# Order of work on four engines: roundings, idle matmuls, row sums and window sums moved in a two-layer attention and convolution kernel

## The chip, the cores and the metric

The kernel runs on one core of a Trainium2 chip. Its time is the device time of one execution in microseconds; the median of several executions is used for comparisons. One more execution is taken with the hardware profiler; its span, from the first to the last instruction, is a little shorter than its time.

## What is computed

Four images of 256 channels by 32 x 32 go through two residual layers, each behind a group normalisation. Layer 0 is attention: 4 heads within windows of 2 x 2 pixels (`hifi`), and 4 heads in which each pixel attends to the 256 pooled windows (`lofi`). Layer 1 is a 3 x 3 convolution of an image that is multiplied by a mask; the mask is made from weighted row and column sums of the image.

```python
qkv = (xw @ h_qkv_w)...                       # window attention, 2 x 2 pixels
attn = softmax(einsum('bghnd,bghmd->bghnm', q, k) * SCALE)
hifi = (attn @ v) @ h_proj_w + h_proj_b
q = xh @ l_q_w; kv = pooled @ l_kv_w          # attention to pooled windows
attn = softmax(einsum('bnhd,bmhd->bhnm', q, k) * SCALE)
lofi = (attn @ v) @ l_proj_w + l_proj_b
x = x + L0(gn(x))
mask = 1 - (|posX - mu_x| + |posY - mu_y|) * mask_weight   # mu from row and column sums
x = x + conv3x3(relu(gn(x) * max(mask, -1))) + bias
```

## The kernel before

Each engine has its own instruction list, written out by hand, and waits on semaphores. SyncE's queue (SP) issues all DMAs. PSUM is held in four pairs of banks: `slot[0]`, `slot[1]`, `slot[2]` for attention, `cps` for the convolution (in the first image, where there is no convolution yet, `cps` serves attention too). Most matrices are multiplied as a high and a low part: ScalarE rounds to the high part, and VectorE or GpSimd subtracts it to give the low part.

For each image b there is a front and a rest. `front(b)` on TensorE: the projection of the local queries; four idle matmuls in image 1 (`keep_warm(WARM[10])`); the pooled keys and values; the window projections with the group means of image b-1 between them; then eight blocks n of local products (`qs` by `ks`, L1180 on), block n into `slot[LA_SLOT[n]]`, from block 3 on only when `la_max` says that the maximum three blocks back is taken. Behind each block stand some matmuls of the previous image's convolution (`conv.more(FRONT[..])`) or, in image 1, idle matmuls on `cps` (`WARM[1 + n]`: 6, 1 and 2 behind blocks 5, 6 and 7). Then follow the turning (a transpose) of the maxima `l_max`, the window sums (`window_scores`, 16 matmuls), the turning of these sums, and the first two score tiles. The convolution of image b-1 begins behind that. `rest(b)` makes the other score tiles, the window values, the head sums (`by_head` with ones), the window output projection, the head products, idle matmuls in image 0 (`WARM[9]`), and the output projection of the local part, which waits for VectorE's product `lnorm` (L917). The convolution of image b-1 fills all gaps from image 1's rest on.

VectorE in a front: the queries' low part (`query_lo`, L771), the keys' low part (`key_lo`, L776, which waits for ScalarE), the row sums (L675) and column sums (L676 to L681) of image b-1, its normalisation (L637 and L610 to L623, behind TensorE's group means), the mask rows (`mask_parts`), the eight maxima (L782), the maxima's high and low parts (`maxima_parts`, L790), the masked images (L722), the first convolution tiles (L736), the window softmax (L799 to L806), more tiles, and the tiles' low parts (L752), for which the convolution waits. In a step: four value products (L885), two adds and a third (L892, L893, L896), the next image's normalisation, transposes (L909), and the product L917.

ScalarE in a front: rectifies the first masked image (L503), copies the window sums to SBUF (L542), rectifies the second, then the softmax's exponential and the tiles' high parts. In image 0's step it takes the exponentials of score tiles 0 to 3 (L520), waits for GpSimd's turned convolution weights (`cw_pool`), rounds two of them (`weight_high`, L461), and then takes the exponentials of tiles 4 to 7.

GpSimd: the window products q by k (L348), which start behind the mask rows of image b-1, the mask sums (L333), and parts of the convolution weights (L374 to L377, and L315 behind ScalarE's two roundings).

## Time and profile before

| | us |
|---|---|
| median of 3 runs (lowest, highest) | 368.33 (368.22, 368.52) |
| profiled execution, its own time | 366.82 |
| its span | 364.9 |
| busy: TensorE, VectorE, ScalarE, GpSimd | 322.0, 280.5, 148.0, 85.8 |
| mean granted TensorE clock, share of full | 0.949 |

A busy TensorE is not one at its peak, since ends of matmuls are modelled. All times of rows are microseconds from the start of the span unless a column says ns. The stretches are: image 0's front and step to about 78 us, image 1's front to about 123, then fronts and steps with the convolution of the previous image between them, some 76 us an image, and from about 305 us the last image's convolution.

### The profile page before, as it was taken

The numbers are of one execution on the slowest core, as the hardware profiler recorded it, in microseconds if no ns is written. First come the engines' busy times: TensorE is split into PE (matmuls) and PEld (weight loads), VectorE is DVE, ScalarE is ACT, GpSimd is POOL, SyncE is SP. The second block draws the span as 40 slices with busy tenths as digits, with TensorE's granted clock in tenths as the row PEclk, the third lists the DMA queues.
The fourth block names the chain that finished last, engine by engine and source line by source line (L and its number), as shares of the span: only waits on it lengthen the run. The fifth ranks groups of instructions, "written<-read, shape, count | busy, mean of one in ns | idle before, by whom it ended". The sixth has DMA issues, their size and how long they took to land.

```text
span 364.9 us, 4118 instructions
## 1 busy us (share of the span) xinstructions
PE 322.0 (88%) x1546; PEld 227.9 (62%) x1546; DVE 280.5 (77%) x518; ACT 148.0 (41%) x186; POOL 85.8 (24%) x47
## 2 busy tenths in 40 slices
PE   1786864999797699998999999998999999979995
PEld 1375542257564485486868773786777836858884
DVE  4979839777867957789897877988879847997662
ACT  2443556345443635535215764453048333031300
POOL 0464948000192020000760020005900200202000
PEclk9999698799968599999899999998999999999999
DMA  8659700007900000029510300098001000101002
GB/s 266 259 81 129 238 5 0 2 0 98 118 2 4 0 2 1 0 82 129 63 38 25 115 3 0 2 169 105 2 4 57 3 0 0 59 0 57 2 0 117
DMA packets 10340, 20.39 MB, mean 56 GB/s; under 512 B 1872, under 2 KB 4816, under 8 KB 10064
## 3 DMA queue, kind: packets, MB, share of 16 engines
q1 hardware_dynamic: 10320, 20.13, 26.8%
q8 instruction: 12, 0.20, 0.2%
q14 instruction: 8, 0.07, 0.1%
HBM read 7.93 MB, written 4.19 MB: 33 GB/s over the span
## 4 chain that ended last, share of the span: by engine, by line
PE 58%; DVE 17%; DMA 8%; ACT 6%; issue 4%; SPq 2%; POOL 2%; DVEq 0%
PE slot L1003 26%; PE cps L1035 16%; PE slot L1079 7%; DMA ks<-probs 4%; PE cps L1003 4%; DMA qs<-probs 3%; ACT probs L520 2%; PE cps L1079 2%; SPq L257 1%; DVE v_lo L752 1%; DVE xn L979 1%; SPq L261 1%; DVE l_max L782 1%; DMA xy<-x 1%; PE slot L1206 1%
## 5 line engine op out<-in xcount | busy, mean ns | idle before, releaser
L348 POOL TENSOR_TENSOR probs<-q_w,k_w 128x1024 f32<-128x1024 f32 x16 | 38.4, 2428 | 115.7 <-DVE rw L715 110.5
L1035 PE MATMUL cps<-v_hi,cw_hi 128*128 128x512 f32 (+1 forms) x144 | 58.6, 407 | 3.8 <-DVE v_lo L752 3.6
L1035 PE MATMUL cps<-v_hi,cw_lo 128*128 128x512 f32 (+1 forms) x144 | 58.4, 406 | 0.0
L1035 PE MATMUL cps<-v_lo,cw_hi 128*128 128x512 f32 (+1 forms) x144 | 57.4, 398 | 0.0
L782 DVE TENSOR_REDUCE l_max<-slot 128x4 f32<-128x1024 f32 x32 | 37.6, 1219 | 7.2 <-PE slot L1003 7.2
L520 ACT ACTIVATE probs<-slot 128x1024 f32<-128x1024 f32 x32 | 31.9, 1023 | 16.8 <-PE slot L1003 16.7
L1035 PEld LDWEIGHTS cps<-v_hi,cw_hi 128*128 128x128 f32 x144 | 28.3, 197 | 14.2 <-ACT v_hi L514 4.3
L1003 PE MATMUL slot<-ks,qs 96*128 96x256 f32 x128 | 24.9, 343 | 10.5 <-DVE l_max L782 4.4
L1035 PEld LDWEIGHTS cps<-v_hi,cw_lo 128*128 128x128 f32 x144 | 28.0, 194 | 6.3 <-issue 0.7
L1035 PEld LDWEIGHTS cps<-v_lo,cw_hi 128*128 128x128 f32 x144 | 28.1, 195 | 4.9
L1003 PEld LDWEIGHTS slot<-ks,qs 96*128 96x128 f32 x128 | 21.8, 236 | 14.4 <-DVE l_max L782 6.7
L503 ACT ACTIVATE xn<-mask 128x1024 f32<-128x1024 f32 x8 | 8.5, 1058 | 45.5 <-DVE mask L722 45.5
L1003 PE MATMUL slot<-xn_hi,w_hi 128*128 128x512 f32 x60 | 24.7, 411 | 2.3 <-DVE xn_lo L650 2.3
L333 POOL TENSOR_TENSOR mask<-rw 128x1024 f32<-128x1024 f32 x8 | 15.2, 1915 | 44.3 <-DVE rw L715 44.3
L1003 PE MATMUL slot<-qs,ks 98*128 98x512 f32 x64 | 21.0, 421 | 5.1 <-ACT probs L520 3.5
L514 ACT CAST v_hi<-mask 128x1024 fp32r<-128x1024 f32 x16 | 16.8, 1049 | 21.0 <-DVE mask L744 11.8
L1003 PE MATMUL slot<-xn_hi,w_lo 128*128 128x512 f32 x60 | 23.9, 398 | 0.0
L1003 PE MATMUL slot<-xn_lo,w_hi 128*128 128x512 f32 x60 | 23.7, 394 | 0.0
L392 POOL TENSOR_TENSOR q_w<-q_w,k_w 128x1024 f32<-128x1024 f32 x3 | 7.2, 2416 | 67.2 <-DVE k_w L885 67.2
L1003 PE MATMUL slot<-probs,cst 128*32 128x512 f32 x176 | 22.8, 657 | 0.0
L752 DVE TENSOR_TENSOR v_lo<-mask,v_hi 128x1024 fp32r<-128x1024 f32 x16 | 19.2, 1224 | 2.3 <-ACT v_hi L514 2.3
L1003 PE MATMUL cps<-cst 128*128 128x384 f32 x44 | 19.7, 602 | 0.0
(188 smaller groups left out, 623.2 us busy)
## 6 DMA issues: line engine op xcount, KB each, us to landing
qs<-probs SPq DMA_DIRECT2D x24, 256.0 KB, 7.5
xy<-x SPq DMA_DIRECT2D x8, 512.0 KB, 8.1
out<-xy SPq DMA_DIRECT2D x8, 512.0 KB, 2.8
raw_cw<-conv_w SPq DMA_DIRECT2D x2, 1152.0 KB, 6.9
ks<-probs SPq DMA_DIRECT2D x12, 128.0 KB, 7.4
probs<-h_qkv SPq DMA_DIRECT2D x2, 192.0 KB, 4.5
probs<-l_kv SPq DMA_DIRECT2D x2, 128.0 KB, 3.9
probs<-selectors SPq DMA_DIRECT2D x1, 256.0 KB, 4.0
```

Source lines behind the costliest of these rows:

```text
L257: sp.dma_start(qs[HD * part:HD * (part + 1), :, n].bitcast(F32), parts[:, n].bitcast(F32)).then_inc(done, 16)
L333: nc.gpsimd.tensor_tensor(mask[:, k].rearrange("p (h w) -> p h w", h=H), rw[:, k, 0].unsqueeze(2).to_broadcast([P, H, W]), rw[:, k, 1].uns ...
L348: nc.gpsimd.tensor_tensor(qk[:, j].rearrange("p (n w) -> p n w", n=NW), q_w[:].rearrange("p (n w) -> p n w", n=NW), k_w[:, j * G:(j + 1) * ...
L392: nc.gpsimd.tensor_tensor(pv[0], pv[0], pv[1], ALU.add).then_inc(pv_pool, 1)
L503: nc.scalar.activation(xn[:, k], mask[:, k], ACT.Relu).then_inc(relu, 1)
L514: nc.scalar.copy(v_hi[:, k, 2 * phase:2 * phase + 2].rearrange("p a b -> p (a b)"), mask[:, k]).then_inc(v_act, 1)
L520: nc.scalar.activation(probs[:, i], flat[score_slot(b, i)], ACT.Exp, scale=SCALE / NW)\
L752: nc.vector.tensor_tensor(v_lo[:, k, part].rearrange("p a b -> p (a b)"), mask[:, k], v_hi[:, k, part].rearrange("p a b -> p (a b)").bitca ...
L782: nc.vector.tensor_reduce(l_max[:, bass.ds(n, HEADS, step=NB)], flat[LA_SLOT[n]].rearrange("p (h m) -> p h m", h=HEADS), AX_X, ALU.max, ne ...
L1003: return nc.tensor.matmul(dst, lhsT, rhs, start=start, stop=stop)
L1035: ins = nc.tensor.matmul(cps[:, pos % 2, y0 * WT:y1 * WT], (cw_hi, cw_hi, cw_lo)[part][:, k, pos, dy + 1, o * P:(o + 1) * P], (v_hi, v_lo, ...
L1079: ins = nc.tensor.matmul(last_bank(o, pos)[:, y0 * WT:y1 * WT], (cw_hi, cw_hi, cw_lo)[part][:, k, pos, dy + 1, o * P:(o + 1) * P], (v_hi, ...
```

## The change

- ScalarE, image 0: the two roundings (`weight_high(1, ...)`, with their wait for GpSimd) follow the exponentials of tiles 4 to 7 instead of preceding them.
- `WARM` is cut to three numbers: 5 at the start, 1 instead of 4 behind image 0's head products, 4 ahead of image 1's pooled keys; those behind the blocks of image 1's front are gone (6, 1 and 2).
- Blocks 5 to 7 of the local products use `slot[0]` and `slot[1]` alone, so each waits for the maximum two blocks back (`LA_FREE`). The window sums go to `slot[2]` (to `cps` in image 0) ahead of the turning of the maxima, which goes to `slot[1]`.
- ScalarE copies the window sums ahead of both rectifications.
- The row sums are an operation of their own (`row_sums`, semaphore `rows_c`): ahead of the keys' low part in image 1's front, behind it in later ones.

```diff
-LA_SLOT = (0, 1, 2, 0, 1, 2, 0, 1)
+LA_SLOT = (0, 1, 2, 0, 1, 0, 1, 0)
+LA_FREE = (0, 0, 0, 1, 2, 4, 5, 6)
-WARM = (5, 0, 0, 0, 0, 0, 6, 1, 2, 4, 4)
+WARM = (5, 1, 4)
...
-                if not first:
-                    rectify(b - 1, 0)
                 act.wait_ge(ssum_pe, b + 1)
-                nc.scalar.copy(q_w[:], flat_cps if first else flat[0]).then_inc(ssum_sb, 1)
-                if not first:
-                    rectify(b - 1, 1)
+                nc.scalar.copy(q_w[:], flat_cps if first else flat[2]).then_inc(ssum_sb, 1)
+                if not first:
+                    for k in range(KT):
+                        rectify(b - 1, k)
...
                     exp_scores(b, range(2, LT - NW))
-                    act.wait_ge(cw_pool, CW_TURNED)
-                    weight_high(1, V_SUM, 2)
-                    weight_high(1, V_DIFF, 0)
...
                 exp_scores(b, range(LT - NW, LT))
+                if first:
+                    act.wait_ge(cw_pool, CW_TURNED)
+                    weight_high(1, V_SUM, 2)
+                    weight_high(1, V_DIFF, 0)
...
-            def line_sums(b, at=slice(0, KT), done=mask_c):
+            def row_sums(b, at=slice(0, KT)):
 
                 carry()
+                n = at.stop - at.start
+                y = img(b, at.start, 0, n * HW).rearrange("p (k h w) -> p k h w", k=n, h=H)
+                nc.vector.tensor_reduce(rc[:, at, 0], y, AX_X, ALU.add).then_inc(rows_c, 1)
...
-                rows = slot[2][0:NB * HEADS, 0, 0:P]
+                rows = slot[1][0:NB * HEADS, 0, 0:P]
...
-                    key_lo(b)
+                    for early in (True, False):
+                        if early == (older is None):
+                            dve.wait_ge(y_ready, b * KT)
+                            row_sums(b - 1)
+                        if early:
+                            key_lo(b)
...
-                        pe.wait_ge(la_max, b * NB + n - 2)
+                        pe.wait_ge(la_max, b * NB + LA_FREE[n])
...
-                    if starting:
-                        keep_warm(WARM[1 + n])
                 if first:
                     pe.wait_ge(qkv_sb, 3)
-                    window_scores(b, cps)
                     pe.wait_ge(zeroed, 1)
+                window_scores(b, cps if first else slot[2])
+                conv.more(FRONT[10])
                 pe.wait_ge(la_max, (b + 1) * NB)
-                nc.tensor.transpose(slot[2][:, 0, 0:P], l_max[:], cst[:, C_ID:C_ID + P]).then_inc(lmt_pe, 1)
-                conv.more(FRONT[10])
-                if not first:
-                    window_scores(b, slot[0])
+                nc.tensor.transpose(slot[1][:, 0, 0:P], l_max[:], cst[:, C_ID:C_ID + P]).then_inc(lmt_pe, 1)
                 conv.more(FRONT[11])
...
                 if first:
-                    keep_warm(WARM[9])
+                    keep_warm(WARM[1])
```

## Rows read from the trace of the kernel before

**Rows 1.** The page, its part on the chain that ended last: shares by engine

```profile
PE 58%; DVE 17%; DMA 8%; ACT 6%; issue 4%; SPq 2%; POOL 2%; DVEq 0%
```

**Rows 2.** The chain in order of time: start us, us, what, count

```profile
63.17 12.06 PE slot L1003 x70
75.23 2.78 PE cps L1003 x8
...
103.61 5.21 PE cps L1003 x12
```

**Rows 3.** VectorE's timeline, step 0: start, us, operation, count, [idle before, releaser]

```profile
59.69 2.85 DVE L893 TENSOR_TENSOR xn<-xn 128x1024 f32<-128x1024 f32 x1
62.57 2.73 DVE L896 TENSOR_TENSOR q_w<-q_w,xn 128x1024 f32<-128x1024 f32 x1
65.23 0.15 DVE L637 COPY gn<-slot 128x4 f32<-128x4 f32 x1
...
69.82 0.72 DVE L909 STREAM_TRANSPOSE v_w<-slot 128x512 f32<-128x512 f32 x1 [1.66 <-PE slot L1003]
...
75.37 1.23 DVE L917 TENSOR_TENSOR k_w<-slot,v_w 128x1024 f32<-128x1024 f32 x1 [1.62 <-PE slot L1003]
```

**Rows 4.** ScalarE's timeline, step 0

```profile
57.78 1.56 ACT L461 CAST cw_hi<-raw_cw 128x768 fp32r<-128x768 f32 x2 [2.39 <-POOL raw_cw L377]
```

**Rows 5.** VectorE's timeline, image 1's front

```profile
87.85 0.42 DVE L776 TENSOR_TENSOR probs<-slot,probs 128x256 f32<-128x256 f32 x1 [2.25 <-ACT lv L478]
88.20 2.28 DVE L675 TENSOR_REDUCE rc<-xy 128x64 f32<-128x2048 f32 x1
...
93.30 0.15 DVE L637 COPY gn<-cps 128x4 f32<-128x4 f32 x1
...
98.85 6.88 DVE L782 TENSOR_REDUCE l_max<-slot 128x4 f32<-128x1024 f32 x6
109.32 2.36 DVE L782 TENSOR_REDUCE l_max<-slot 128x4 f32<-128x1024 f32 x2 [3.60 <-PE slot L1003]
...
112.62 2.34 DVE L722 SCALAR_TENSOR_TENSOR mask<-mask,xn 128x1024 f32<-128x1024 f32 x2
...
117.40 0.29 DVE L799 TENSOR_REDUCE s_max<-slot 128x32 f32<-128x128 f32 x1 [1.16 <-PE slot L1206]
```

**Rows 6.** TensorE's and GpSimd's timelines, image 1's front

```profile
92.61 0.28 PE L1003 MATMUL cps<-mv,cst 128*128 128x4 f32 x2
122.64 0.77 PE L1035 MATMUL cps<-v_hi,cw_hi 128*128 128x512 f32 x1 [3.57 <-DVE v_lo L752]
...
99.10 9.29 POOL L348 TENSOR_TENSOR probs<-q_w,k_w 128x1024 f32<-128x1024 f32 x4 [34.88 <-DVE rw L715]
108.35 3.78 POOL L333 TENSOR_TENSOR mask<-rw 128x1024 f32<-128x1024 f32 x2
```

**Rows 7.** VectorE's and TensorE's timelines, image 2's front and the values behind

```profile
187.35 0.28 DVE L790 CAST probs<-slot 32x128 fp32r<-32x128 f32 x1 [0.42 <-PE slot L1196]
193.92 0.29 DVE L799 TENSOR_REDUCE s_max<-slot 128x32 f32<-128x128 f32 x1 [1.57 <-PE slot L1206]
...
188.63 1.94 PE L1003 MATMUL slot<-probs,cst 128*32 128x512 f32 x16
207.32 0.74 PE L1003 MATMUL slot<-p_w,sel 128*128 128x512 f32 x2 [0.26 <-ACT p_w L556]
```

**Rows 8.** TensorE's timeline, one block of four local products by itself

```profile
100.12 1.23 PE L1003 MATMUL slot<-ks,qs 96*128 96x256 f32 x4 [2.01 <-DVE l_max L782]
```

**Rows 9.** TensorE by stretches: stretch, its length, busy (instructions), granted clock, DMA, GB/s

```profile
62.00:64.00 2.00, 0.84 (x7) 0.50 0.00 0
68.00:70.00 2.00, 2.00 (x17) 0.84 0.00 0
...
174.00:175.00 1.00, 1.00 (x9) 0.72 1.11 125
177.00:178.00 1.00, 1.00 (x4) 0.57 1.03 117
```

More of the change, by code:

```diff
@@ L189, in build @@
         mask_last = [sem(f"mask_last{k}") for k in range(KT)]
+        rows_c = sem("rows_c")
         mask_c, soft_c, pool_c = sem("mask_c"), sem("soft_c"), sem("pool_c")
@@ L659, in pooling, with column_sums @@
                 link(nc.vector.tensor_tensor(pool_lo[:], pool_s, pool_hi[:].bitcast(F32), ALU.subtract))
-            def line_sums(b, at=slice(0, KT), done=mask_c):
+            def row_sums(b, at=slice(0, KT)):
                 carry()
+                n = at.stop - at.start
+                y = img(b, at.start, 0, n * HW).rearrange("p (k h w) -> p k h w", k=n, h=H)
+                nc.vector.tensor_reduce(rc[:, at, 0], y, AX_X, ALU.add).then_inc(rows_c, 1)
+            def column_sums(b, at=slice(0, KT), done=mask_c):
                 n = at.stop - at.start
@@ L674, in line_sums @@
                 w = HW // 2
-                nc.vector.tensor_reduce(rc[:, at, 0], y.rearrange("p k (h w) -> p k h w", h=H), AX_X, ALU.add)
                 link(nc.vector.tensor_tensor(t[:, :, 0:w], y[:, :, 0:w], y[:, :, w:2 * w], ALU.add))
@@ L688, in mask_parts @@
                 dve.wait_ge(link.sem, link.base + 1)
+                dve.wait_ge(rows_c, b + 1 + at.start)
                 g, sums, parts, m = gn[1][:, :, at], rc[:, at], rw[:, at], mu[:, at]
@@ L838, in masks @@
             def masks(b):
-                dve.wait_ge(y_ready, (b + 1) * KT)
-                line_sums(b)
+                column_sums(b)
                 normalisation(b, 1)
@@ L934, in last_front @@
                 conv_result(older, (V_LEFT, V_RIGHT))
-                line_sums(b, slice(0, 1), mask_last[0])
+                row_sums(b, slice(0, 1))
+                column_sums(b, slice(0, 1), mask_last[0])
                 mask_parts(b, slice(0, 1), mask_last[0])
@@ L941, in last_front @@
                 conv_tiles(b, 0, 0)
-                line_sums(b, slice(1, 2), mask_last[1])
+                row_sums(b, slice(1, 2))
+                column_sums(b, slice(1, 2), mask_last[1])
                 conv_low(b, 0, 0)
@@ L1132, in front @@
                 if starting:
-                    keep_warm(WARM[10])
+                    keep_warm(WARM[2])
                 pe.wait_ge(pool_c, (b + 1) * N_POOL)
```

3 lines of the change are left out of this document (1 added, 2 removed).

## The prediction

> **What bounds the kernel now.** I read the shares of the chain that ended last first [rows 1]: TensorE has 58% of it and VectorE 17%, so an edit pays where the chain leaves TensorE's real work. Then the same chain in order of time [rows 2]. From image 1's convolution on (about 123 us) it is almost only TensorE; before that it holds three pieces that compute nothing: idle matmuls of 2.78 us at 75.23 and 5.21 us at 103.61, and ScalarE's last exponentials at 59 to 63 us, which stand behind two weight roundings. The timelines of the engines there [rows 3 to 6] say what is late next when such a piece goes, and those of the third image's front [rows 7] what a later turning of the maxima costs where TensorE is full.
>
> The profiled execution took 366.82 us, 1.51 us less than the median of the runs, 368.33 us. Sums are made on it; the 1.51 us are added at the end.
>
> **Maxima in two bank pairs, first image.** Blocks 5, 6 and 7 of the local products now wait for the maxima two blocks back instead of three. A block alone at the low clock takes 1.23 us [rows 8], and one maximum 1.15 us (6.88 by six, [rows 5]); so the maxima stay nearly gapless, but by my estimate from these two the last block ends about 0.9 us later than with a pair to spare, and so do the window sums behind it, at a mostly low clock. The clock rises while they run, so their end moves by less. I take +0.55 us for all that follows; bounds 0 (the sums hidden) and +2 (the clock rises a good while later, since TensorE has more holes).
>
> **Roundings after the exponentials.** The exponential of tile 3 ends at 55.4 (57.78 less the wait of 2.39 us for GpSimd's turned weights); ScalarE rounds for 1.56 [rows 4], and does tiles 4 to 7 until the head sums can begin at 63.17 [rows 2]. So four exponentials took 3.8 us (59.3 to 63.1). Now tile 4 follows at once, from 55.4 + 0.55, and the last ends near 59.9, with 0.1 us for scores that come between value products: 3.2 us earlier. The roundings run from 59.9 to 61.5, GpSimd's low parts after them. They were cover for nothing: nobody needs them before image 1's convolution.
> What is late next? On TensorE the head sums, the projection and the head products took 12.06 us from 63.17 [rows 2]; from 60.0 they end at 72.1 at worst, near 70.5 if the clock comes back sooner. On VectorE: an add with two SBUF inputs beside GpSimd took 2.85 and 2.73 us [rows 3], against 1.17 for such an operation alone (2.34 by two, [rows 5]). The first add, now at 60.2, is alone (1.2), the second from 61.5 is beside the moved low parts (2.7), ending at 64.2. From the normalisation's start at 65.23 to the product at 75.37 there are 10.14 us, of which 1.66 and 1.62 are waits for TensorE [rows 3]: 6.86 of work, so the product could start at 71.1 and end at 72.2. I take VectorE's 71.1; TensorE's worst end would cost 1.0 more.
>
> **Idle matmuls.** After the head products 4 become 1: 2.78 us become 0.7, which end before 72.2. Before, TensorE began the output projection at 78.0, when the idle matmuls ended [rows 2]; now it begins at 72.2. Together with the exponentials: -5.7 us. The four ahead of the pooled projections stay. In image 1's front nine go, six of them as 5.21 us [rows 2].
>
> **Row sums, image 1.** VectorE waited 2.25 us for ScalarE before the keys' low part; the row sums behind it took 2.28 less the overlap, 2.2 us [rows 5]. They now fill that gap, so the column sums start 2.2 us earlier against TensorE. But the normalisation behind them needs the group means, which TensorE makes at 92.61 to 92.9 [rows 6], behind its projections, and VectorE got there at 93.30 [rows 5]. So 0.4 us is gained and the rest becomes a wait. The low part comes at most 0.3 us later, and with it the stacking DMAs on SP's queue; I price that at 0 (below by the maxima, which bound the blocks anyway) to 0.3. In later images the row sums keep their place: 0. The first maximum thus moves from 98.85 to 92.8.
>
> **Maxima of image 1.** Six maxima in 6.88, a wait of 3.60 on the idle matmuls, two more in 2.36 [rows 5]: ended at 111.7. Now eight in 9.2 plus two waits of 0.17 for a cold block: 102.4, 9.3 us earlier. It doesn't all arrive. GpSimd's products (9.29 us) start behind the mask rows and its mask sums (3.78) behind them [rows 6]; they shift by only 6.1, to 102.3 and 104.2 / 106.1. The first masked image so runs beside the second mask sum, which it did not before. Beside GpSimd such an operation took 2.7 to 2.85, not 1.17 [rows 3, 5]: first masked image 104.3 to 107.0, second to 108.2, tiles 1.25 more, softmax from 109.45. Its turned sums are there by 106, since ScalarE's copy no longer follows the first rectification; before, VectorE stood 1.16 us for them until 117.40 [rows 5]. From there to the first convolution matmul at 122.64 [rows 6] is 5.24: now 114.7, which is -8.0 us.
> The Trainium skill (GPSIMD Engine Reference, 8. Key points) says that GpSimd contends with VectorE instructions that have two SBUF inputs. By it the masked image is slowed and the maxima, which read PSUM, are not; were the masked image not slowed, the convolution would start at 113.8 and the sum would be 0.8 us better. The trace agrees on the adds [rows 3]; a masked image beside a mask sum is in no row.
> The clock at 114.7 is low, as it was at 122.64; how long it stays so can differ: -1 to +1.4, I take 0.
>
> **Window sums ahead of the turned maxima, images 2 and 3.** TensorE saves a short wait before the turning. But the turning now comes behind 1.9 us of window sums [rows 7] and six convolution matmuls (about 1.4 us: they ended at 188.63, where the sums began, and were under way at 187.35), so the maxima's parts, which VectorE began at 187.35, begin near 190.2, and VectorE stands there meanwhile: the masked images are queued behind. Against that it no longer stands 1.57 us before the softmax [rows 7], whose inputs are now early. Net +1.25 us for all behind the softmax: VectorE's tiles and low parts, ScalarE's roundings and exponentials, the turned weights. There is no slack to take it: TensorE waited 0.26 us for ScalarE's weights at 207.32 [rows 7]. So +1.25 us in each of images 2 and 3; bounds 0 and +2.9 (nothing of the second wait returned). The maxima's DMAs leave 2.9 us later too, which costs TensorE a wait of about 0.7 us at the first scores, inside the same 1.25. In the last image nothing but the split of the line sums changes: 0.
>
> **Sum:** -8.0 + 1.25 + 1.25 = -5.5, so 361.3 profiled and 362.8 us median.
>
> **Rivals.** (a) The late maxima cost nothing, because TensorE has room for them, or a clock that stays up over the wait for the keys' DMA [rows 9] gives it back: -8.0, 360.3 us. For: the clock was low there from about 174.4 to 177.9 (means 0.72 and 0.57 at its ends), which costs half of that, 1.7 us per image, and where it falls may depend on where the wait lies. Against: TensorE already waits on the very chain that is delayed [rows 7].
> (b) The clock takes part of the early gain: +2 instead of +0.55 in the first image and +1.4 at the first convolution matmuls. -2.6, 365.7 us.
> (c) The exponentials don't come earlier, because scores or values bind them. Then their part of -5.7 shrinks to the idle matmuls' 1.4: -1.2, 367.1 us. Against it: what ended ScalarE's wait there is GpSimd, not TensorE [rows 4].
> (d) Slower. The idle matmuls held the clock. Places: first image +2; the wait before the output projection, behind which TensorE would run at half speed for as long as from 62 us to 68.6, where the clock came back [rows 9], so 6.6 us (+3.3); convolution start +1.4; the new waits of images 2 and 3 ahead of their convolutions (+1.7 to +3.4 each, 1.7 taken). Of the first 0.55 is in the sum already: -5.5 + 1.5 + 3.3 + 1.4 + 3.4 = +4.1, 372.4 us. It decides from 5.5 us of loss, that is 11 us more of dense matmul work at 1.2 GHz. For: the clock fell to its lower level behind short waits at 62 and at 174 us [rows 9]. Against: around the output projection TensorE is full on both sides and idle for about one microsecond only.
> The Trainium skill (TensorE: Matmul & The Clock Gate, Part 4) says that transposes in TensorE's own mode don't count as busy. By it the nine turnings of image 1's front don't keep the clock, which is case (b)'s second half, 364.2 us with that alone. No row shows a stretch of turnings alone.
>
> **Chances.** Forecast with its bounds 0.58; (a) 0.12; (b) 0.15; (c) 0.06; (d) 0.09. The range reaches over (a) and (b), with the term bounds in between: 359.3 to 366.0. Below 0.2% a measurement of this kernel can't tell a change from none; only the edge of (c) lies there. Faster 0.87, same 0.04, slower 0.09.
>
> **What would show it.** Last exponential of step 0 near 60 us; the second of the two adds long, the first short; product near 71 and output projection near 72; row sums just before the keys' low part, then a wait of some 1.5 us before the normalisation; eight maxima in one run near 93 to 102.5; the first of the two masked images over 2 us; first convolution matmul near 114.7; in images 2 and 3 about 3 us of VectorE standing before the maxima's parts and TensorE waiting about 1.3 us before the next convolution. I am wrong if the masked images of image 1 are held by something else than GpSimd, if image 2 loses nothing, or if the granted clock between 72 and 92 us leaves its full level.

## The result and the profile after

| | before | after |
|---|---|---|
| median, us | 368.27 (4 runs, 367.26 to 368.52) | 372.43 (4 runs, 372.22, 372.29, 372.57 and 1042.99) |
| profiled execution, us | 366.82 | 372.29 |
| its span, us | 364.9 | 370.2 |
| mean granted clock | 0.949 | 0.931 |

The ratio after to before is 1.0142 (95%: 1.0103 to 1.0181): slower, where faster was forecast. The median of after is of all four executions, without the one of 1042.99 us it is 372.29; here and below the ratios leave out executions over 1.5% above the fastest of their kernel. The chain's shares by engine, against [rows 1]:

```profile
PE 53%; DVE 24%; DMA 10%; ACT 6%; issue 4%; SPq 3%; DVEq 0%; ACTq 0%
```

TensorE has fewer points of the chain, VectorE has seven more and DMA two. Where the span's 5.3 us came in, by the same events in both traces (before, then after; the value products are VectorE's first of an image):

| stretch | before | after | difference |
|---|---|---|---|
| start to ScalarE's copy of image 0's window sums | 45.61 | 47.38 | +1.77 |
| from there to the output projection | 32.23 | 27.48 | -4.75 |
| from there to image 1's value products | 54.65 | 56.02 | +1.37 |
| to image 2's value products | 75.61 | 79.18 | +3.57 |
| to image 3's | 75.60 | 78.93 | +3.33 |
| to the end | 81.2 | 81.2 | 0.0 |

So the first three rows together are still a small gain, -1.6 us, where -8.0 was forecast; the images 2 and 3 lost 6.9 us, where 2.5 was forecast.

**Image 0's step.** VectorE's, ScalarE's and GpSimd's timelines of after (start, us, operation, count, [idle before, releaser]), then from the view of the tile `cw_lo` the shortest, median and longest of GpSimd's low parts in ns, then TensorE's timeline, against [rows 2, 3, 4]:

```profile
61.46 1.22 DVE L905 TENSOR_TENSOR xn<-xn 128x1024 f32<-128x1024 f32 x1
62.71 1.23 DVE L908 TENSOR_TENSOR q_w<-q_w,xn 128x1024 f32<-128x1024 f32 x1
63.85 0.15 DVE L639 COPY gn<-slot 128x4 f32<-128x4 f32 x1
64.04 1.63 DVE L612 TENSOR_TENSOR gn<-gn 128x2 f32<-128x2 f32 x1
65.71 1.77 DVE L613 SCALAR_TENSOR_TENSOR gn<-gn 128x2 f32<-128x2 f32 x1
67.51 0.17 DVE L614 TENSOR_SCALAR gn<-gn 128x2 int32<-128x2 int32 x1
...
73.59 1.21 DVE L929 TENSOR_TENSOR k_w<-slot,v_w 128x1024 f32<-128x1024 f32 x1
...
56.13 5.12 ACT L522 ACTIVATE probs<-slot 128x1024 f32<-128x1024 f32 x5 [0.35 <-PE slot L1017]
61.14 1.57 ACT L463 CAST cw_hi<-raw_cw 128x768 fp32r<-128x768 f32 x2
...
62.84 4.62 POOL L317 TENSOR_TENSOR cw_lo<-raw_cw,cw_hi 128x768 fp32r<-128x768 f32 x2 [3.33 <-ACT cw_hi L463]
...
L317 POOL TENSOR_TENSOR cw_lo<-raw_cw,cw_hi x6: 1835/1859/2812, 23.3 to 65.6; 128x768 fp32r<-128x768 f32 x6
...
70.69 0.91 PE L1017 MATMUL cps<-cst 128*128 128x384 f32 x2
74.86 3.78 PE L1017 MATMUL slot<-k_w,w_out 128*128 128x512 f32 x4 [3.26 <-DVE k_w L929]
```

The exponentials end at 61.25, although image 0 ran 1.8 us late, and the roundings follow them, as meant. The adds, which GpSimd held before (2.85 and 2.73), now take 1.22 and 1.23 us: the first is alone, and the second began 0.13 us ahead of GpSimd's work. But GpSimd's moved low parts (62.84 to 67.46) fall on image 1's normalisation: two operations on 128x2 numbers, 0.16 us each in the profile before, take 1.63 and 1.77 us, and each ends as one of GpSimd's two instructions ends (62.84 and 2.81, the longest, give 65.65; 62.84 and 4.62 give 67.46). So the product comes at 73.59, and TensorE, which has one idle matmul left, stands 3.26 us before the output projection. What that did to the clock (view by stretches: length, busy of TensorE, its weight loads, VectorE, ScalarE and GpSimd, granted clock, DMA, GB/s):

```profile
72.00:73.00 1.00, 0.00 (x0) 0.00 (x0) 1.00 (x4) 1.00 (x2) 0.00 (x0) 1.00 0.00 0
73.00:74.00 1.00, 0.00 (x0) 0.00 (x0) 1.00 (x3) 1.00 (x2) 0.00 (x0) 0.89 0.00 0
74.00:76.00 2.00, 1.14 (x2) 0.62 (x3) 2.00 (x3) 2.00 (x4) 0.00 (x0) 0.50 0.00 0
...
78.00:80.00 2.00, 2.00 (x5) 1.27 (x4) 1.32 (x4) 0.00 (x0) 0.00 (x0) 0.50 0.00 0
...
81.00:82.00 1.00, 1.00 (x6) 0.77 (x5) 0.97 (x2) 0.00 (x0) 0.00 (x0) 1.00 0.00 0
```

TensorE was idle from 71.6, and at 73.8 the clock fell from 2.4 to 1.2 GHz and came back at 80.6. The output projection took 3.78 us instead of 1.88 before; in the profiles below where the clock stayed up it took 1.88 to 1.99. It began 3.0 us earlier than before, and the projection of the queries behind it ended at about the same time as before (82.2 against 82.4): the gain was gone. This is the profiled execution; below, the same kernel's second profile shows no such fall here.

**Image 1's front**, against [rows 5, 6]:

```profile
84.63 2.28 DVE L668 TENSOR_REDUCE rc<-xy 128x64 f32<-128x2048 f32 x1
...
87.70 0.43 DVE L784 TENSOR_TENSOR probs<-slot,probs 128x256 f32<-128x256 f32 x1 [0.79 <-ACT lv L480]
...
92.78 0.16 DVE L639 COPY gn<-cps 128x4 f32<-128x4 f32 x1 [1.75 <-PE cps L1017]
...
98.34 5.74 DVE L790 TENSOR_REDUCE l_max<-slot 128x4 f32<-128x1024 f32 x5
104.26 2.36 DVE L790 TENSOR_REDUCE l_max<-slot 128x4 f32<-128x1024 f32 x2 [0.18 <-PE slot L1017]
106.80 1.23 DVE L790 TENSOR_REDUCE l_max<-slot 128x4 f32<-128x1024 f32 x1 [0.18 <-PE slot L1017]
111.82 0.28 DVE L798 CAST probs<-slot 32x128 fp32r<-32x128 f32 x1 [3.79 <-PE slot L1209]
...
112.34 2.34 DVE L730 SCALAR_TENSOR_TENSOR mask<-mask,xn 128x1024 f32<-128x1024 f32 x2
...
115.88 0.28 DVE L807 TENSOR_REDUCE s_max<-slot 128x32 f32<-128x128 f32 x1
...
106.70 4.82 PE L1017 MATMUL slot<-probs,cst 128*32 128x512 f32 x16
111.45 0.33 PE L1209 MATMUL slot<-cst,l_max 128*128 128x128 f32 x1
...
121.10 0.77 PE L1049 MATMUL cps<-v_hi,cw_hi 128*128 128x512 f32 x1 [3.67 <-DVE v_lo L760]
...
107.86 3.77 POOL L335 TENSOR_TENSOR mask<-rw 128x1024 f32<-128x1024 f32 x2
```

The row sums are ahead of the keys' low part, and the normalisation waits 1.75 us for the group means. The eight maxima run almost without a gap and end at 108.0 instead of 111.7. But the window sums now stand between the last block and the turning, and at the low clock they take 4.82 us; VectorE stands 3.79 us before the maxima's parts, and of 3.7 us 1.5 are left at the softmax and at the first convolution matmul (121.10 against 122.64).

**Image 2's front**, against [rows 7, 9]: TensorE, then VectorE, then one stretch of the view by stretches.

```profile
173.07 2.93 PE L1017 MATMUL slot<-ks,qs 96*128 96x256 f32 x12 [2.79 <-DMA ks<-probs]
...
187.51 1.94 PE L1017 MATMUL slot<-probs,cst 128*32 128x512 f32 x16
...
190.89 0.27 PE L1209 MATMUL slot<-cst,l_max 128*128 128x128 f32 x1
...
191.19 0.28 DVE L798 CAST probs<-slot 32x128 fp32r<-32x128 f32 x1 [3.47 <-PE slot L1209]
...
195.91 0.28 DVE L807 TENSOR_REDUCE s_max<-slot 128x32 f32<-128x128 f32 x1
...
174.00:178.00 4.00, 4.00 (x16) 3.54 (x15) 3.49 (x3) 0.00 (x0) 4.00 (x2) 0.50 0.59 71
```

The order of sums and maxima did what was forecast in kind: counted from the start of the span, parts begin 3.84 us later and the softmax 1.99 us later than before (forecast 2.9 and 1.25). Something else was not forecast: the first block of products waited 2.79 us for the keys' DMA (1.79 before; in image 3, 3.92 against 1.79), and the stretch of low clock behind it, 174.4 to 177.9 before, lasts from 172.8 to 179.6, twice as long. Counted from the end of the keys' low part on VectorE to that first block, the two images took 9.32 and 9.32 us before, 10.32 and 11.45 us after. In image 1, where no output is stored meanwhile, the same way took 7.36 us in both kernels.

### The profile page after: what moved, and what is told of

Its sections match the earlier page's. It is cut to its first block, busy times and chain, and to the rows that moved or that the text cites. A ratio compares the mean times of both kernels' runs of the same rounds, so it can differ in the third digit from the quotient of the medians.

```text
span 370.2 us, 4071 instructions
## 1 busy us (share of the span) xinstructions
PE 319.7 (86%) x1522; PEld 226.4 (61%) x1522; DVE 280.3 (76%) x518; ACT 148.8 (40%) x186; POOL 85.6 (23%) x47
## 4 chain that ended last, share of the span: by engine, by line
PE 53%; DVE 24%; DMA 10%; ACT 6%; issue 4%; SPq 3%; DVEq 0%; ACTq 0%
PE slot L1017 26%; PE cps L1049 16%; PE slot L1093 7%; DMA ks<-probs 5%; DMA qs<-probs 4%; ACT probs L522 2%; PE cps L1093 2%; DVE l_max L790 2%; DVE mask L730 2%; SPq L259 2%; PE cps L1017 2%; DVE v_lo L760 1%; DVE xn L993 1%; DMA xy<-x 1%; DVE mask L745 1%
## 5 line engine op out<-in xcount | busy, mean ns | idle before, releaser
L1049 PE MATMUL cps<-v_hi,cw_hi 128*128 128x512 f32 (+1 forms) x144 | 59.4, 413 | 5.1 <-DVE v_lo L760 3.7
L1017 PE MATMUL slot<-ks,qs 96*128 96x256 f32 x128 | 25.9, 348 | 15.7 <-DMA ks<-probs 7.8
L1017 PE MATMUL slot<-xn_hi,w_hi 128*128 128x512 f32 x60 | 26.0, 434 | 2.6 <-DVE xn_lo L652 2.6
L1017 PE MATMUL slot<-xn_lo,w_hi 128*128 128x512 f32 x60 | 24.5, 409 | 0.0
L542 ACT COPY q_w<-slot 128x1024 f32<-128x1024 f32 x3 | 3.0, 1015 | 38.0 <-PE slot L1017 38.0
L837 DVE SCALAR_TENSOR_TENSOR xy<-slot,bias,xy 128x256 f32<-128x256 f32 x32 | 13.2, 474 | 5.7 <-PE slot L1017 5.7
```

Of the source, the lines that this page charges most:

```text
L837: last = nc.vector.scalar_tensor_tensor(dst, flat[s][:, n * G:(n + 1) * G].rearrange("p (hg wg) -> p hg wg", hg=HG), bias[:, k:k + 1], dst ...
L1017: return nc.tensor.matmul(dst, lhsT, rhs, start=start, stop=stop)
L1049: ins = nc.tensor.matmul(cps[:, pos % 2, y0 * WT:y1 * WT], (cw_hi, cw_hi, cw_lo)[part][:, k, pos, dy + 1, o * P:(o + 1) * P], (v_hi, v_lo, ...
```

## The experiments

All are compared with the kernel before on the same chip. Where the periods of low clock fall differs from execution to execution, so that one kernel's times spread by one or two per cent (before: 364.3 to 371.2 us). I therefore use, beside medians, the intervals between the value products of images 1, 2 and 3 in the profiled execution, which spread less: for the kernel after 79.2 and 78.9 in one profile, 78.8 and 78.6 in the other. Each run has one profile. "Way of the keys" is the time from the keys' low part to the first block in images 2 and 3.

| run | ratio to before (95%) | interval 1 to 2, 2 to 3 | way of the keys |
|---|---|---|---|
| before | 1 | 75.6, 75.6 | 9.32, 9.32 |
| after | 1.0142 (1.0103 to 1.0181) | 79.2, 78.9 | 10.32, 11.45 |
| e0_after_again | 1.0144 (1.0109 to 1.0178) | 78.8, 78.6 | 10.14, 11.15 |
| e1_nine_back | 1.0087 (1.0062 to 1.0112) | 76.1, 76.6 | 9.16, 9.58 |
| e2_four_back | 0.9973 (0.9942 to 1.0003) | 75.9, 77.1 | 9.21, 9.64 |
| e3_only_idle_cut | 1.0028 (0.9986 to 1.0069) | 78.6, 78.4 | 11.03, 10.77 |
| e4_only_roundings | 0.9944 (0.9900 to 0.9988) | 75.5, 75.6 | 9.30, 9.38 |
| e5_sums_behind | 1.0056 (1.0025 to 1.0087) | 78.1, 78.7 | 10.45, 11.20 |
| e7_low_parts_later | 1.0011 (0.9977 to 1.0044) | 79.1, 78.4 | 10.32, 10.95 |
| e8_three_pairs_first | 1.0028 (0.9994 to 1.0061) | 79.3, 76.5 | 10.46, 10.52 |
| e9_fill_12 | 1.0030 (1.0003 to 1.0058) | 76.8, 76.5 | 9.31, 9.35 |
| e10_before_fill_52 | 1.0552 (1.0502 to 1.0602) | 78.1, 78.6 | 10.57, 11.24 |
| e12_three_mended | 0.9850 (0.9775 to 0.9925) | 76.8, 76.5 | 9.37, 9.36 |
| e11_four_mended | 0.9776 (0.9699 to 0.9854) | 75.7, 75.3 | 9.38, 9.36 |
| e13_no_fill | 0.9947 (0.9912 to 0.9982) | 79.0, 78.7 | 10.48, 11.29 |
| e14_sums_ahead | 0.9875 (0.9819 to 0.9931) | 76.8, 76.6 | 9.35, 9.35 |
| e15_sums_behind_all | 0.9881 (0.9843 to 0.9918) | 75.7, 75.3 | 9.40, 9.36 |
| e16_fill_behind_image0 | 0.9875 (0.9808 to 0.9942) | 76.7, 76.5 | 9.24, 9.43 |
| e17_fill_and_sums_behind | 0.9807 (0.9759 to 0.9856) | 75.6, 75.2 | 9.34, 9.41 |

### The change again, and its idle matmuls

The kernel after, unchanged, in a new comparison:

> The changed kernel itself, beside the kernel before on the same chip. Executions of the kernel before spread here from 364.6 to 371.0 us. If the loss of 4.2 us of the first comparison belongs to the change, the ratio is again near 1.014. If a good part of it was where the clock happened to fall in those executions, the ratio is between 1.000 and 1.008.

371.13 us, ratio 1.0144: the loss belongs to the kernel, not to one set of executions. But this profile loses it in another way. The small operations of the normalisation are held as before (1.62 and 1.77 us), yet TensorE waits only 1.56 us for the product, because a low clock at 64.8 to 68.2 us had already delayed its head products, and the clock is up from there to 98.9:

```profile
77.31 1.98 PE L1017 MATMUL slot<-k_w,w_out 128*128 128x512 f32 x4 [1.56 <-DVE k_w L929]
```

Image 1's value products begin at 129.30 us, 3.2 us ahead of the kernel before; images 2 and 3 then lose 6.2 us. So what both profiles of the changed kernel share is the loss in images 2 and 3 (6.9 and 6.2 us), not the fall of the clock before the output projection. Over all 19 profiles the clock fell there in the four where TensorE waited 3.23 to 3.26 us (after and the runs e5, e8 and e9), and in none of the fifteen where it waited 1.56 us or less.

The three idle matmuls behind image 0's head products put back, and the nine of image 1's front:

```diff
-WARM = (5, 1, 4)
+WARM = (5, 4, 4)
```

> The kernel after with four idle matmuls instead of one behind the head products of image 0. Clock theory (TensorE's wait of 3.26 us before the output projection drops the clock, and 2.8 us are lost in the projections behind): the clock stays full to 97 us, the end is 2 to 3 us earlier, 369.5 to 370.5. Rival (the wait itself is all that counts): no change, 372.4.

```diff
                     conv.more(FRONT[2 + n])
+                    if starting:
+                        keep_warm((0, 0, 0, 0, 0, 6, 1, 2)[n])
```

> The kernel after with the nine idle matmuls behind blocks 5 to 7 of image 1 put back. Clock theory (cutting idle matmuls lowers the clock for the window sums of image 1, which took 4.82 us instead of 1.94): the sums take about 2 us again, but the idle matmuls delay the last two maxima to about 111.5, so nothing is gained or lost: 372.4 within 0.7. Rival (the nine were pure cost): 3 us slower, 375.5.

366.31 and 370.51 us. With the three back the clock stays up through the output projection:

```profile
76.00:78.00 2.00, 2.00 (x7) 1.12 (x6) 2.00 (x2) 2.00 (x4) 0.00 (x0) 1.00 0.00 0
```

That looked like rival (d) at one place, but it is not an effect of the three: in the repeated run without them the clock stayed up as well, and the two profiles have the same times to image 1's first convolution matmul (119.96 and 119.99 us). The table says that most of both gains is elsewhere: the two intervals together are 153.0 and 152.8 us instead of 158.1, in images 2 and 3, where neither edit changes anything. For the nine the account nearly closes: their own cost, from the output projection to image 1's value products, is 55.3 us against 52.0 in the repeated run, +3.3, and the two intervals are 4.7 us shorter than that run's 157.4: -1.4, where the two ratios say -2.1 us. So these runs do not tell the clock from something that changes with the number of instructions ahead. Neither expectation was met: the first was to take 369.5 to 370.5 us and took 3.2 less, and the second was to leave 372.4 or cost 3 us and gained 1.9. The nine did bring image 1's window sums back to 1.94 us, but the first convolution matmul then came at 122.79.

### One part alone on the kernel before

```diff
-WARM = (5, 0, 0, 0, 0, 0, 6, 1, 2, 4, 4)
+WARM = (5, 0, 0, 0, 0, 0, 0, 0, 0, 1, 4)
```

> The kernel before with only the idle matmuls cut (one behind the head products, none behind the blocks). Clock theory: output projection 1.3 us earlier, maxima of image 1 end 3.5 us earlier, but window sums at the low clock give most of it back: -0.5 to -2 us, 366.3 to 367.8. Theory that the cut is the main loss: slower than before by 2 us or more, above 370.3.

```diff
-                    act.wait_ge(cw_pool, CW_TURNED)
-                    weight_high(1, V_SUM, 2)
-                    weight_high(1, V_DIFF, 0)
                 ...
                 exp_scores(b, range(LT - NW, LT))
+                if first:
+                    act.wait_ge(cw_pool, CW_TURNED)
+                    weight_high(1, V_SUM, 2)
+                    weight_high(1, V_DIFF, 0)
```

> The kernel before with only the two roundings moved behind the exponentials. Theory: last exponential near 59.4, the next image's normalisation then runs beside GpSimd's low parts and takes 5.3 us instead of 2.3, the four idle matmuls hold the clock, and the product at 75.37 comes 2 to 3 us earlier: 365.5 to 366.5. Rival (the order of the roundings is itself the loss, through GpSimd's contention): no gain or a loss, 368.3 or more.

The cut of the idle matmuls alone brings image 1's first convolution matmul from 122.64 to 119.59 and gives it all back behind: the intervals are 3.0 and 2.8 us longer, although no instruction of images 2 and 3 was touched. The median of 368.25 us was 0.5 above the expected range. The roundings alone gain (365.17 us, 0.9944, 0.3 us below the expected range) and leave the intervals as they were, although they too move GpSimd's low parts onto the normalisation (1.62 and 1.78 us there).

### The three suspects in the kernel after

Window sums of images 2 and 3 behind the turned maxima again (those of images 0 and 1 stay ahead):

```diff
-                window_scores(b, cps if first else slot[2])
-                conv.more(FRONT[10])
+                ahead = first or starting
+                if ahead:
+                    window_scores(b, cps if first else slot[2])
                 pe.wait_ge(la_max, (b + 1) * NB)
                 nc.tensor.transpose(slot[1][:, 0, 0:P], l_max[:], ...)
+                conv.more(FRONT[10])
+                if not ahead:
+                    window_scores(b, slot[2])
```

> The changed kernel with the window sums of images 2 and 3 behind the turned maxima again. Order theory: the softmax of these images comes about 1.2 us earlier in each against the blocks in front of it, so 2.4 us less than the changed kernel. Rival (later images have slack, their loss is the keys' DMA and the clock): no difference, below 0.5 us.

GpSimd's low parts behind image 1's first normalisation:

```diff
                 pool.wait_ge(cw_act, 6)
+                pool.wait_ge(gn_c[0], 2 * N_GN)
                 link(weight_low(nc.gpsimd, 1, V_SUM, 2), 0)
```

> The changed kernel with GpSimd's two low parts of the weights waiting for the end of image 1's first normalisation. Contention theory (they held two small operations of that normalisation for 1.63 and 1.77 us): the normalisation takes 2.3 us again, product L929 near 70.5 instead of 73.6, TensorE's wait before the output projection below 1 us where it was 3.26, and the clock doesn't fall there: 3 to 5 us less than the changed kernel. Rival (the clock falls there anyway): the product is early, but the end moves by less than 1.5 us.

Three bank pairs for image 0's maxima, as before the change:

```diff
+LA_SLOT0 = (0, 1, 2, 0, 1, 2, 0, 1)
+LA_FREE0 = (0, 0, 0, 1, 2, 3, 4, 5)
```

> The changed kernel with three bank pairs for the blocks of image 0 alone. If thinner blocks kept the clock low there until 46.5 us instead of 44.7, the copy of the window sums comes 1.5 us earlier (45.7 against 47.4) and the end 1 to 1.8 us earlier. Rival (the fall of the clock there is chance): the copy comes 0.3 to 0.6 us earlier on average, and the end too.

369.47, 365.91 and 368.57 us: each gives back a part (ratios 1.0056, 1.0011, 1.0028 against 1.0144), none all. Against the repeated run that is 1.7, 5.2 and 2.6 us less, where 2.4, 3 to 5 and 1 to 1.8 were expected. Their profiles do not show where the medians gained: image 1's value products begin at 130.46, 128.90 and 128.74 us against 129.30 in the repeated run, and the intervals of the first are 78.1 and 78.7, only 0.7 shorter and 0.1 longer, with the clock low for 3.4 us more in image 3. The small operations of the normalisation are as short as before again once GpSimd works later (VectorE's, then GpSimd's timeline of the second of the three):

```profile
66.38 0.16 DVE L613 TENSOR_TENSOR gn<-gn 128x2 f32<-128x2 f32 x1
66.57 0.16 DVE L614 SCALAR_TENSOR_TENSOR gn<-gn 128x2 f32<-128x2 f32 x1
...
68.67 3.65 POOL L317 TENSOR_TENSOR cw_lo<-raw_cw,cw_hi 128x768 fp32r<-128x768 f32 x2 [8.50 <-DVE gn L626]
```

The product comes 1.1 us earlier than in the repeated run and the wait before the output projection falls from 1.56 to 0.57 us, but the profiled execution, the longest of the ten, ends only 0.1 us earlier (369.73 against 369.87 us). Seven of the ten take 364.5 to 367.1 us with a mean granted clock of 0.944 to 0.948, where all six of the changed kernel had 0.930 to 0.935. So the 1.3% between the two ratios, 4.9 us, comes with a higher clock in executions that no profile shows; that it is the earlier normalisation that keeps it up is argued, not shown. For image 0 I compared all profiles: from its first maximum to the copy of its window sums, with two pairs 11.7 to 12.7 us in seven profiles (mean 12.3), with three pairs 9.9 to 11.9 in eleven (mean 10.7; the one that begins 14 us late left out). Two pairs cost about 1.6 us there.

### The way of the keys: TensorE's instruction fetch

What images 2 and 3 lost lies between the keys' low part and the first block, in transfers that the change did not touch. The trace shows one thing that moved. TensorE's instructions come by a DMA queue of their own, q8, in fetches of 16 KB, each for 256 instructions (12 fetches for some 3,050 matmuls and weight loads in the trace of after). The change takes 12 idle matmuls, 48 instructions, out ahead of image 2. Before, a fetch came at 158.05 us, 3.2 us ahead of ScalarE's copy of the local queries, which starts a burst of stacking transfers and the store of an output; after, it came 0.9 us behind the copy (160.54), in the first microseconds of the burst, and in image 3 2.3 us behind it. The view of DMA over 12 us from the burst's start, before, then after: queues (packets, MB, share of 16 engines), then issues with KB and median us to landing.

```profile
q1 hardware_dynamic: 1088, 1.87, 98.0%
...
out<-xy SPq DMA_DIRECT2D x1, 512.0 KB, 3.0
...
q1 hardware_dynamic: 1136, 1.96, 103.3%
q8 instruction: 1, 0.02, 0.6%
...
out<-xy SPq DMA_DIRECT2D x1, 512.0 KB, 4.4
```

The same store takes 4.4 us instead of 3.0 to land when the fetch falls beside it, and the stacking transfers queue behind. Twelve narrow matmuls (their results are not used) at the start put the count of instructions back:

```diff
             keep_warm(WARM[0])
+            fill(12)        # 12 matmuls of 4 columns on cps
```

> The changed kernel with 12 narrow matmuls (4 columns) at the very start, where TensorE waits for image 0's normalisation: the same number of TensorE instructions as before the change, and no work where the idle matmuls were. Fetch theory (with 12 matmuls fewer, TensorE's 16 KB instruction fetch falls at 1 to 2.5 us behind the start of ScalarE's copy of the local queries, into the stacking DMAs of images 2 and 3, where it was 3.3 us ahead): the lag from the keys' low part to the first block goes back from 10.1 to 11.4 us to 9.3, and the end is 2 to 4 us earlier than the changed kernel, 367.5 to 369.5. Rival (the slower DMAs have another cause): same lag and 371.5.

The same tried the other way round, on the kernel before: 52 narrow matmuls move its fetches back by 208 instructions, which is forward by 48, onto the burst.

> The kernel before with 52 narrow matmuls at the same place: with 256 instructions to a fetch, this puts its fetches where 12 matmuls fewer would. Fetch theory: the lag of images 2 and 3 rises from 9.3 to 10 us or more, and the end is 1.5 to 4 us later than before, 368.5 to 371. Rival: no change, 366.9.

Both answered. The first takes 368.16 us, 3.0 less than the repeated run and as expected, and brings the way of the keys to 9.31 and 9.35 us and the intervals to 76.8 and 76.5. The second makes them 10.57 and 11.24 and lengthens the intervals by 2.5 and 3.0 us in the kernel that had not changed otherwise; its median of 387.36 us, where 368.5 to 371 was expected, is no measure, as the 52 themselves delayed image 0 by some 14 us. Its DMA view from the burst's start:

```profile
q8 instruction: 1, 0.02, 0.5%
...
out<-xy SPq DMA_DIRECT2D x1, 512.0 KB, 4.7
```

Over all 19 profiles the place of the fetch sorts the way of the keys: where it comes 3.3 to 2.7 us ahead of the copy, the way is 9.3 to 9.4 us and the store lands in 2.96 to 3.00; between 0.03 us ahead of the copy and 0.3 us behind, 9.2 to 9.6 and 3.2 to 3.7 us; 0.9 to 2.3 us behind, 10.1 to 11.5 and 4.3 to 5.4 us. The burst's first packet moves 1.03 to 1.06 us behind the copy in every profile, and the fetches of the middle group had ended by 0.97 to 1.36 us behind it: they were nearly over when the burst began.

What a late way costs depends on the clock. In the run with three bank pairs, image 3's fetch is in the burst and TensorE waits for the keys as long as in the others:

```profile
250.43 1.69 PE L1019 MATMUL slot<-ks,qs 96*128 96x256 f32 x12 [2.99 <-DMA ks<-probs]
```

but here the clock stayed up through the whole interval, which is 76.5 us, as with the twelve narrow matmuls and a wait of 1.81. Everywhere else a fetch in the burst went with 6.8 us of low clock in the interval to image 2 and 3.4 or 6.8 us in that to image 3; without one these are 0 or 3.4 us.

### All of it mended, and the order by itself

The low parts later, three pairs in image 0 and the twelve narrow matmuls together, with the window sums ahead, and with those of images 2 and 3 behind:

> The changed kernel with GpSimd's low parts behind the normalisation, three bank pairs in image 0, and the 12 narrow matmuls; window sums stay ahead of the turned maxima. If the three costs add up (5, 2.5 and 3 us singly, with overlap): 362 to 365. Rival (they repair the same loss): 366.

> As the run before it, and with the window sums of images 2 and 3 behind the turned maxima. Order theory: 1.2 us less in each of two images, 2.4 us below the run with three mended. Rival (slack in those images): no difference.

360.30 and 362.11 us (four executions each), both faster than before. The first is below its expected 362 to 365; the second is 1.8 us above the first, where 2.4 below was expected. The intervals say that the late maxima cost 1.15 and 1.2 us; the medians said the contrary, and it was also open what the fetch is worth by itself. So three more: the first kernel without the twelve, and both again with more executions.

> The kernel after with GpSimd's low parts behind the normalisation and three bank pairs in image 0, but without the twelve narrow matmuls at the start. Theory (instruction fetch): TensorE's 16 KB instruction fetch falls 1 to 2.5 us behind ScalarE's copy of the local queries again, in the stacking burst; from the end of the keys' low part to the first block of products 10.2 to 11.5 us in images 2 and 3 instead of 9.36, with the longer low clock behind it. So 2 to 4 us slower than the same kernel with the twelve, some 362.5 to 364.5 us. Rival (the twelve only moved the clock): 9.3 to 9.4 us in both images and 0.5 to 1 us faster than with the twelve, some 359.5 us.

> The same three mendings with the twelve narrow matmuls, window sums ahead of the turned maxima as in the kernel after, in more executions: median 359.5 to 362, keys' wait 9.3 to 9.4 us; interval from image to image (value matmuls of images 1, 2, 3) 76.5 to 76.9 us.

> As the run before, with the sums of images 2 and 3 behind the turned maxima. Theory (the late maxima cost 1.15 us an image): intervals 75.3 to 75.7 us, and a median 2 to 2.4 us below that of the run before, 357.5 to 359.5. Rival (the order costs nothing, the difference of the intervals seen was the clock's): intervals and medians within 0.5 us of each other.

365.85 (12 executions), 365.35 (six, at two levels: 360.1, 360.4 and 364.6 to 366.5) and 362.47 us (six, 358.8 to 362.8). The intervals of the two kernels that were run again repeat to 0.1 us. They are 79.0 and 78.7 us without the twelve, 76.8 and 76.6 with them, and 75.7 and 75.3 with the old order of sums and maxima. So the fetch is worth 2.2 us in each of the two images, of which up to 1.7 is the clock, low for 3.4 us less in each; the order is worth 1.2. But the twelve at the start had a price of their own: they put a fetch, at 27 us, into image 0's burst, which had been free of one. TensorE's first block in images 0 and 2, without and with the twelve:

```profile
32.35 1.70 PE L1020 MATMUL slot<-ks,qs 96*128 96x256 f32 x12 [0.58 <-DMA ks<-probs]
...
167.71 2.93 PE L1020 MATMUL slot<-ks,qs 96*128 96x256 f32 x12 [2.95 <-DMA ks<-probs]
...
35.21 2.93 PE L1020 MATMUL slot<-ks,qs 96*128 96x256 f32 x12 [3.19 <-DMA ks<-probs]
...
170.79 2.63 PE L1020 MATMUL slot<-ks,qs 96*128 96x256 f32 x12 [1.82 <-DMA ks<-probs]
```

The wait for the keys' DMA goes from 0.58 to 3.19 us in image 0 and from 2.95 to 1.82 in image 2 (3.76 to 1.82 in image 3). These two are the extremes: over all profiles the way of the keys in image 0 is 9.2 to 10.1 us in the five with a fetch at 27 us and 7.8 to 9.1 in the fourteen without, the waits 1.9 to 3.2 and 0 to 2.2. So it is probably the same effect in a third place, of one to two microseconds, and a part of the reason why the median gained so little. Six narrow matmuls behind image 0's idle matmul instead:

```diff
                     keep_warm(WARM[1])
+                    fill(6)
```

> The kernel after with GpSimd's low parts behind the normalisation, three bank pairs in image 0, and six narrow matmuls behind image 0's idle matmul instead of twelve at the start. Theory (instruction fetch, the only thing that the twelve changed for the better): the six shift the fetches of images 2 and 3 to about 1 us ahead of the burst, 9.2 to 9.6 us from the keys' low part to the first block there, and leave image 0 without a fetch in its burst: its wait for the keys' DMA 0.6 us instead of 1.9 to 3.2 with the twelve. Intervals 76.5 to 76.9 us, median 361 to 363.5, 2 to 4 us below the same kernel without them. Rival (image 0's longer wait is the start's clock): a wait of 2 to 3 us there too, no gain over twelve at the start.

> The run before with the sums of images 2 and 3 behind the turned maxima. Late maxima at 1.15 us an image: intervals 75.3 to 75.7 us, 2.3 us below the run before in the median, 359 to 361. Rival: the late maxima cost nothing in the median, the clock gives it back: within 0.5 us of the run before.

```profile
33.38 1.70 PE L1020 MATMUL slot<-ks,qs 96*128 96x256 f32 x12 [1.37 <-DMA ks<-probs]
...
166.65 2.71 PE L1020 MATMUL slot<-ks,qs 96*128 96x256 f32 x12 [1.81 <-DMA ks<-probs]
```

364.05 and 360.11 us (six executions each, 358.8 to 369.2 and 356.3 to 361.2). Image 0's wait is 1.03 and 1.37 us, images 2 and 3 keep the short way. The expected waits in image 0 were 0.6, so part of it is something else. The median with the sums ahead missed its range by 0.6 us, that with the sums behind was within it; the medians of the three runs before had all come out above theirs, by 1.4 to 3.4 us, with the intervals and the way of the keys as expected. Over all 16 executions of the three runs with sums ahead (e12, e14, e16) the mean is 363.4 us, over the 16 of the three with sums behind 360.9: 2.6 us, where two intervals of 1.2 give 2.4. The executions that the ratios count give less, 361.7 and 360.5 us, and the pair with the twelve and six executions each has nearly the same ratio (0.9875 and 0.9881). So 1.2 us an image is what the intervals show; the whole time agrees in sign only. The last kernel takes 1.9% less than before (0.9759 to 0.9856) and has the lowest median of all.

## Why the prediction was wrong

**Exponentials ahead of the roundings: right.** Forecast 3.2 us earlier; they ended 1.85 us earlier with image 0 1.77 us late, so 3.6. Alone, with the four idle matmuls kept, the edit gains about 2 us (0.9944).

**What is late next on VectorE: wrong, and this step carried the largest term, -5.7 us.** The low parts were taken to slow the second add by 1.5 us. That add had begun 0.13 us before them and kept its 1.23 us, and they held two operations of the normalisation by 1.47 and 1.61 us. The sum used 6.86 us of work from the normalisation to the product; it was 9.74 (63.85 to 73.59). My row for the price was of large operations and I looked for large operations in the path; a small one pays the same, because what it waits for is the end of GpSimd's instruction. The trace of before had such a row in image 0, a 128x2 operation of 0.53 us that ends with GpSimd's second instruction (VectorE's, then GpSimd's timeline):

```profile
26.48 0.53 DVE L990 SCALAR_TENSOR_TENSOR mwf<-mwf 128x2 f32<-128x2 f32 x1
23.13 3.86 POOL L315 TENSOR_TENSOR cw_lo<-raw_cw,cw_hi 128x768 fp32r<-128x768 f32 x2
```

The Trainium skill (SBUF — State Buffer, Terms) says that the port pair of VectorE and GpSimd is locked for a full instruction and that the loser fully blocks. The trace agrees: the two small operations end at 65.67 and 67.48, where GpSimd's instructions end; by the forecast's rule of a slowed second operation they would have cost nothing.

**Idle matmuls: wrong by the clock.** They were priced as time of TensorE alone, 2.8 us to 0.7. With the late product TensorE stood 3.26 us instead of about one, the clock fell in the profiled execution and the stretch to the queries' projection took 2.8 us more (82.2 less 74.86, against 82.4 less 77.84). The forecast named the sign for this, the clock leaving its full level between 72 and 92 us, and the place and size of it in rival (d), +3.3. In the second profile of the same kernel the clock fell earlier instead, at 51.2 and 64.8 us, and not here; the loss in time was the same.

**Image 0's two pairs: the term was right in kind and too small**, +0.55 against +1.77 in the profile and +1.6 in the mean of all. It had the bound of +2.

**Row sums: right.** Normalisation 0.5 us earlier (0.4), and a wait of 1.75 us (about 1.5).

**Image 1's maxima: right as a run, wrong in what follows.** Eight maxima in 9.7 us (9.5 forecast). But I priced the window sums ahead of the turning in images 2 and 3 only and left them out here, where they take 4.82 us at the low clock (3.91 in the repeated run): a term put at nothing. With them, the masked images begin at 112.34, when GpSimd is done, and are not slowed at all (2.34 us for two); the part of the forecast on masked images beside GpSimd did not come to a test. Of -8.0 us at the first convolution matmul -1.5 were left: of the 6.5 us between, 5.5 were already missing at the first maximum (98.34, forecast 92.8).

**Images 2 and 3: the term of +1.25 us each held to 0.15 us** (1.10 to 1.30 in three pairs of profiles; the repeated run and e5, both with the fetch in the burst, give 0.7 and -0.1), with its signs: VectorE stood 3.47 us before the parts, and TensorE 0.46 us at the first scores and 0.54 us in the convolution behind (forecast 0.7 and about 1.3). But the loss was 3.6 and 3.3 us, because 2.2 us each came from a resource that was in no row of mine and so stood in the sum at nothing: instruction fetch, with the longer low clock behind it. It is the largest piece of the gap, and the one that both profiles of the kernel show.

**The sum.** Forecast -5.5; measured +5.3 in the span. The gap of 10.8 us, by the stretches of the first table: image 0 1.2 (1.77 less 0.55); from there to the output projection 1.5 (4.75 us gained, where 5.7 and the 0.55 were forecast); the projections at the low clock 2.8; image 1's front otherwise 0.9 (-1.4 for -2.3); images 2 and 3 4.4 (6.9 less 2.5), the fetch. Rival (d) gave 372.4 us, and 372.43 was measured, but that is partly chance: its first two places were right in the profiled execution (+1.5 and +3.3 against 1.2 and 2.8), the second of them not in the repeated one; the start of the convolution did not cost its 1.4, and in images 2 and 3 a low clock did cost about what was priced, but behind the wait for the keys' DMA, not behind the new waits that (d) named.

## What to carry to other kernels

When an edit moves work on GpSimd, list every two-input operation of VectorE in the new window, the smallest too: here each was held to the end of a GpSimd instruction. An idle matmul is also a number of instructions: after adding or removing any on a full TensorE, look in the new trace at where its instruction fetches fall against the DMA bursts of later stages. And compare changes of under 1% by intervals between like events in the profiles beside medians, which here spread with the clock.

## What the runs showed of the hardware

- An instruction fetch of TensorE (16 KB) in the first microseconds of a burst made an output store of 512 KB land in 4.3 to 5.4 us instead of 3.0, delayed the first block's keys by 1 to 2 us, and with the longer low clock behind the wait cost 2.2 us a time; in the one interval where the clock stayed up it cost nothing. At 0.3 us behind the copy or earlier the store landed in 3.7 us or less. The page after counts the fetches:

```profile
q8 instruction: 12, 0.20, 0.2%
```

The Trainium skill (Runtime: NRT & Kernel Launch, Instruction fetch mechanics) says that an engine fetches blocks of 256 instructions by its own DMA queue and that the cost of this is mostly hidden. The trace agrees with the blocks. No run here shows a cost of the fetches outside the bursts; those in the bursts of images 2 and 3 were not hidden (2.2 us an image), and there the measurement decides. That the delay comes from the DMA engine that carries the fetch is my reading; no run shows it.

- VectorE operations on 128x2 numbers with two inputs in SBUF took 1.62 to 1.78 us beside GpSimd in eight profiles (seven kernels) and 0.5 to 0.7 in image 0, each ending within 0.03 us of a GpSimd instruction, and 0.16 without it.
- After, TensorE was idle from 71.6 us, its clock fell at 73.8 and came back at 80.6, 5.8 us of it on dense work; in the second profile of the same kernel, with a wait of 1.56 us there, it did not fall. The time of one kernel (window sums ahead, the twelve narrow matmuls) had two levels, 360.1 and 360.4 us at a mean granted clock of 0.952, and 364.6 to 366.5 at 0.925 to 0.936.
